# Attention's end, the pair products and the inverse root of a fused graph-attention kernel: another order of transfers and products, a shorter root

## The chip, the cores and the metric

One core of a Trainium2 chip. The metric is the device time of one execution, in microseconds (us): the median of 3 runs for the kernel before.

## The reference

With N = 4096 nodes and D = 512 features, `adj` a sparse 0/1 matrix [N, N], everything in fp32:

```python
q, k, v = x @ Wq.T + bq, key @ Wk.T + bk, value @ Wv.T + bv
s = (q @ k.T / N ** 0.5) * adj
s = where(abs(s) < 1e-5, -1e9, s)
x1 = layernorm(x + softmax(s) @ v @ Wm.T + bm)          # eps 1e-5
out = layernorm(x1 + relu((adj @ x1) @ W.T + b))        # eps 1e-5
```

`layernorm` subtracts the row's mean and divides by sqrt(variance + eps).

## The kernel before, in words

All products are made of 16-bit halves (a value is split in a high and a low part, three or two matmuls stand for one exact one). Node rows are worked in tiles of 128, n = 0 to 31. The program is written out by hand: every engine has its own instruction list, and semaphores tie them together. SP (`@block.sync`) and POOL (`@block.gpsimd`) issue the transfers, in the order in which they are written; a wait in such a list holds up all that stands behind it.

**Attention** takes 64 steps: 32 over the first half of the keys, then 32 over the second half (g = 32 + n). A step makes scores (L830), masks them and finds the row maximum (VectorE), takes exponentials and splits them in `Phl` (ScalarE, the high half, L1146; VectorE, the low half, L1529). SP turns both halves into `PT` by transposing transfers (`turn_prob`, L365 and L368) and TensorE weighs the values with them (`weigh`, L850). In the second half the two half results are merged, turned (`turn_merged`, L475 and L478) and projected (`project`, L871); the row is normalised to x1, split, turned (`turn_x1`, L462 and L465), stored (`store_x1`, L453), and multiplied with W1 (`rows_product`, L885), which gives the row Y[n]. `turn_x1(n)` waits until TensorE has used the turned row before it (semaphore `y_mm`). The adjacency is stored again in bf16 as it goes by (`store_adj`).

**Aggregation** makes adj @ Y for pairs of tiles (p, p + 16), p = 0 to 15. An adjacency tile (p, k) is 128 rows of 4096, turned from DRAM into SBUF in one transposing transfer (`adj_tile`, L483). Pairs 0 and 1 are made plainly (`aggregate`, L945, 64 matmuls a tile), pairs 2 to 15 with seven block products of 16 matmuls each instead of eight (`seven`, `product`, L976): VectorE makes four sums of adjacency blocks (`adj_sum`, L1892) and combines the products (`taken`, L1899, and `together`, L1904), and signed sums of Y rows (`Ta`, `Tb`) are made beforehand. `output` (L1847, L1851, L1854) and `result` (L1858 to L1863) then make the last layernorm of each tile.

**The order around the change.** POOL loads the rows of Y back in seven chunks of 4 tiles, 1 MB each (`load_y`), and the signed sums in three loads of 2, 2 and 1.5 MB (`load_sums`). Chunks 4, 5 and 6 wait for the last scores (`s_mm`), chunks 2 and 3 for the eleventh signed sums in DRAM; the first two sums loads for the last weighting (`o_mm`), the third for row 31's product (`y_mm`). In SP's last attention step (n = 31) tiles (0, 0) and (0, 1) stand ahead of `turn_prob`. After the loop come the last x row, row 29's turn, tile (1, 0), the last merged row, row 30's turn, the bias, tile (1, 1), row 31's turn.

TensorE's own list at attention's end is: `weigh(63)`, `rows_product(28)`, `project(62)`, the first parts of `aggregate(0, 0)` (32 matmuls), `rows_product(29)`, `project(63)`, 16 matmuls, `rows_product(30)`, 32 matmuls, `rows_product(31)`, then 176 matmuls for the rest of pairs 0 and 1, and `seven`. `seven` of the first pair waits until the fourth plain output has been read from PSUM (`f_out`). VectorE, after row 31's product, makes the last five signed sums (`joined`, `last_sums`, `signed_low`), three plain outputs with their results, four `adj_sum`, and the fourth output.

The inverse root is made on [128, 1] columns: three opening steps (add eps, a bit trick, scale) and three rounds of three instructions (L1608, L1610, L1611), 12 steps in all. In attention the steps are spread between VectorE's larger instructions (`score_chunks`); for the last rows and in `result` they run one behind the other.

In a pair, TensorE makes the products in the order 0, 1, 2, 3, 4, 5, 6. VectorE finishes the first tile's output after product 4 and the second tile's after product 6:

```python
dve.wait_ge(s_prod, 7 * q + 5)
taken(q, 5, csum[:, 1, :], u5[:, :], ps[:, 4, :], ALU.add)
output(u, 0, cs[:, 0, :], q + PLAIN)
result(u, 0)
dve.wait_ge(s_prod, 7 * q + 7)
taken(q, 7, csum[:, 0, :], u5[:, :], ps[:, 6, :], ALU.add)
taken(q, 9, u3[:, :], u2[:, :], ps[:, 6, :], ALU.add)
taken(q, 10, csum[:, 1, :], u3[:, :], ps[:, 5, :], ALU.subtract)
output(u + 1, 1, cs[:, 1, :], q + PLAIN)
```

## Time and profile before

| | |
|---|---|
| median of 3 runs | 2120.08 us (2117.37 to 2121.25) |
| the profiled execution | 2123.79 us |
| its span in the profile | 2122.1 us |
| TensorE busy | 2049.1 us, 97% |
| VectorE busy | 1487.2 us, 70% |
| ScalarE busy | 675.2 us, 32% |
| moved by the DMA engines | 359.57 MB, mean 169 GB/s |
| TensorE's slices below 9 tenths | 1st, 4th, 32nd and 40th (7 each), 34th (8) |

Times in the profile count from the start of the span. Matmuls are pipelined, so a busy TensorE need not be at its peak; a matmul's recorded duration is longer than the distance to the next one, and a group of matmuls is read by its length over its count. PEclk is the granted TensorE clock as a share of 2.4 GHz. In a timeline the bracket gives the idle time before an instruction and what ended it. [...]

### The profile page before, as it was taken

To read this page: it belongs to the slowest core of one execution; us is meant where nothing else is said; L and a number is where in the kernel's file an instruction comes from. 1 tells how busy PE (TensorE), PEld (TensorE's weight loads), DVE (VectorE), ACT (ScalarE), POOL (GpSimd) and SP (SyncE) were. 2 spreads that over 40 slices of the span, in tenths; PEclk is the share of its full clock that TensorE was granted. 3 is DMA by queue.
4 is the path that set the end of the run, shared out by engine and by line. 5 is a ranking of instruction groups with operands and counts; after the bars stand their busy time and mean duration, and the time that the engine had idled before them with its cause. 6 is when DMAs were issued, how large, how long until landed. Compare 5 with 4: busy or idle time off the path is not lost.

```text
span 2122.1 us, 30051 instructions
## 1 busy us (share of the span) xinstructions
PE 2049.1 (97%) x9471; PEld 981.9 (46%) x9471; DVE 1487.2 (70%) x3540; ACT 675.2 (32%) x884; POOL 81.1 (4%) x139
## 2 busy tenths in 40 slices
PE   7997999999999999999999999999999798999997
PEld 6773444444444444444444444444444333444443
DVE  3876656656565665687777777778888457888887
ACT  3443434344343434343333333343434110000000
POOL 1110000000000000000000000000000000000000
PEclk9998999999999999999999999999999899999999
DMA  7676777676667676887766666677777975555551
GB/s 243 230 267 150 189 176 155 168 168 162 162 161 182 148 173 155 224 168 163 164 163 160 163 165 165 162 176 184 187 185 208 256 174 119 134 124 119 133 138 56
DMA packets 586290, 359.57 MB, mean 169 GB/s; under 512 B 500992, under 2 KB 505088, under 8 KB 585856
## 3 DMA queue, kind: packets, MB, share of 16 engines
q1 hardware_dynamic: 564672, 275.07, 51.5%
q0 software_dynamic: 21568, 83.89, 16.3%
q8 instruction: 24, 0.39, 0.1%
q14 instruction: 26, 0.21, 0.0%
HBM read 181.15 MB, written 88.60 MB: 127 GB/s over the span
## 4 chain that ended last, share of the span: by engine, by line
PE 90%; DVE 5%; SPq 2%; DMA 2%; issue 1%; ACT 1%; DVEq 0%; ACTq 0%
PE ps L830 31%; PE ps L850 30%; PE ps L976 16%; PE ps L885 4%; PE ps L871 4%; PE ps L791 3%; SPq L483 1%; DMA wc<-in_L_gnn_Wv 1%; DMA x1T<-x1hl 1%; PE ps L775 1%; PE ps L945 0%; PE ps L738 0%; DMA stg<-in_L_gnn_value 0%; PE ps L804 0%; DVE mcol L1368 0%
## 5 line engine op out<-in xcount | busy, mean ns | idle before, releaser
L850 PE MATMUL ps<-V,PT 128*128 128x512 f16 x3072 | 676.3, 380 | 12.4 <-issue 12.4
L830 PE MATMUL ps<-KT,thl 128*128 128x512 f16 x3072 | 677.8, 381 | 9.6 <-DVE thl L1473 9.6
L850 PEld LDWEIGHTS ps<-V,PT 128*128 128x128 f16 x3072 | 301.1, 98 | 377.4 <-issue 17.2
L830 PEld LDWEIGHTS ps<-KT,thl 128*128 128x128 f16 x3072 | 301.5, 98 | 375.6 <-DVE thl L1473 10.7
L1500 DVE SCALAR_TENSOR_TENSOR prob<-ps,c_now,adjh 128x512 f32<-128x512 f32 x256 | 192.1, 751 | 289.1 <-PE ps L830 287.1
L1133 ACT ACTIVATE small<-prob 128x512 f32<-128x512 f32 x256 | 161.1, 630 | 631.4 <-DVE prob L1500 342.3
L1529 DVE SCALAR_TENSOR_TENSOR Phl<-prob,Phl 128x2048 f16<-128x2048 f32 x64 | 146.6, 2291 | 77.4 <-ACT Phl L1146 77.4
L1513 DVE CUSTOM_DVE_ANT_0 prob<-prob,small 128x512 f32<-128x512 f32 x256 | 174.5, 683 | 0.0
L1138 ACT ACTIVATE prob<-prob,nbias,inv 128x2048 f32<-128x2048 f32 x64 | 134.1, 2095 | 102.9 <-DVE nbias L1522 102.9
L1506 DVE TENSOR_SCALAR small<-small,eps_s,neg_s 128x512 f32<-128x512 f32 x256 | 139.0, 543 | 21.0 <-ACT small L1133 21.0
L1146 ACT ACTIVATE Phl<-prob 128x2048 f16<-128x2048 f32 x64 | 122.3, 1910 | 7.1
L1296 ACT ACTIVATE p<-ps 128x512 f32<-128x512 f32 x14 | 8.4, 597 | 335.5 <-DVE csum L1899 212.2
L976 PE MATMUL ps<-Y,AT 128*128 128x512 f16 x448 | 101.0, 384 | 6.4 <-DVE y L1847 6.4
L791 PE MATMUL ps<-xT,Aq 128*128 128x512 f32 x384 | 97.0, 403 | 1.8 <-DVE xT L1308 1.8
L885 PE MATMUL ps<-W1T,x1T 128*128 128x512 f16 x384 | 90.3, 386 | 6.6 <-DMA x1T<-x1hl 6.6
L871 PE MATMUL ps<-Wvm,UT 128*128 128x512 f16 x384 | 88.1, 379 | 1.1 <-issue 1.1
L672 POOL DMA_DIRECT2D adjh<-in_adj x64 | 36.1, 564 | 1388.5 <-DMA adj_bf<-adjh 826.6
L976 PE MATMUL ps<-Ta,S 128*128 128x512 f16 x336 | 79.4, 379 | 0.0
L976 PE MATMUL ps<-Tb,S 128*128 128x512 f16 x336 | 79.4, 379 | 0.0
L791 PEld LDWEIGHTS ps<-xT,Aq 128*128 128x128 f32 x384 | 71.1, 191 | 16.6 <-DVE xT L1308 2.5
L976 PEld LDWEIGHTS ps<-Y,AT 128*128 128x128 bf16 x448 | 44.2, 99 | 61.0 <-issue 9.5
L885 PEld LDWEIGHTS ps<-W1T,x1T 128*128 128x128 f16 x384 | 38.1, 99 | 53.7 <-DMA x1T<-x1hl 7.1
(179 smaller groups left out, 1765.1 us busy)
## 6 DMA issues: line engine op xcount, KB each, us to landing
adjh<-in_adj POOLq DMA_DIRECT2D x64, 512.0 KB, 5.3
adj_bf<-adjh SPq DMA_DIRECT2D x64, 512.0 KB, 4.4
t_in<-t_dram SPq DMA_DIRECT2D x64, 256.0 KB, 2.9
x_in<-in_x SPq DMA_DIRECT2D x64, 256.0 KB, 4.2
stg<-in_L_gnn_value POOLq DMA_DIRECT2D x12, 1024.0 KB, 7.3
rows<-in_x SPq DMA_DIRECT2D x32, 256.0 KB, 4.1
t_dram<-tq POOLq DMA_DIRECT2D x8, 1024.0 KB, 9.0
o_dram<-z_out SPq DMA_DIRECT2D x32, 256.0 KB, 2.8
```

Source lines behind the costliest of these rows:

```text
L791: last = nc.tensor.matmul(ps[:, BT + e, :], Aq[:, m, k, e * P:(e + 1) * P], xT[:, b, s, k, :], start=(n == 0), stop=(n == 3 * KD - 1))
L830: last = nc.tensor.matmul(ps[:, BS + c, :], thl[:, b, s, k * P:(k + 1) * P], KT[:, m, k, c * C:(c + 1) * C], start=(n == 0), stop=(n == 3 ...
L850: last = nc.tensor.matmul(ps[:, BU + b, :], PT[:, b, s, m, :], V[:, v, m, :], start=(m == 0 and q == 0), stop=(m == MT - 1 and q == 2))
L871: last = nc.tensor.matmul(ps[:, BZ, :], UT[:, b, s, k, :], Wvm[:, m, k, :], start=(n == 0), stop=(n == 3 * KD - 1))
L885: last = nc.tensor.matmul(ps[:, BY, :].rearrange("p (o n) -> p o n", n=P), x1T[:, s, k, :], W1T[:, m, :, k, :], start=(q == 0), stop=(q == ...
L976: last = nc.tensor.matmul(ps[:, bank, :].rearrange("p (s d) -> p s d", s=2), left(m), right(m), start=(m == 0), stop=(m == NP - 1))
L1133: nc.scalar.activation(small[:, c % 2, :], prob[:, b, c * C:(c + 1) * C], ACT.Abs).then_inc(s_abs, 1)
L1138: nc.scalar.activation(prob[:, b, :], prob[:, b, :], ACT.Exp, bias=nbias[:, b:b + 1], scale=inv[:, 0:1], accum_out=rsum[:, b:b + 1]).then_ ...
L1500: nc.vector.scalar_tensor_tensor(out=prob[:, b, c * C:(c + 1) * C], in0=ps[:, BS + c, :], scalar=c_now[:, b:b + 1], in1=adjh[:, b, c * C:( ...
L1506: nc.vector.tensor_scalar(small[:, c % 2, :], small[:, c % 2, :], eps_s[:, 0:1], neg_s[:, 0:1], ALU.is_lt, ALU.mult).then_inc(s_neg, 1)
L1513: nc.vector.tensor_tensor_reduce(out=prob[:, b, c * C:(c + 1) * C], in0=prob[:, b, c * C:(c + 1) * C], in1=small[:, c % 2, :], scale=1.0, ...
L1529: nc.vector.scalar_tensor_tensor(out=Phl[:, b, LO, :], in0=prob[:, b, :], scalar=P_SCALE, in1=Phl[:, b, HI, :], op0=ALU.mult, op1=ALU.subt ...
```

## The change

In SP's list, tile (0, 1) goes from before the last `turn_prob` to behind the last x row's load; tile (1, 0) from before the last merged row's turn to behind row 30's turn and store; row 31's turn and store go ahead of tile (1, 1). In POOL's list, chunks 4, 5 and 6 of Y wait for the last turned probabilities instead of the last scores, the first sums load for the last projection, the second for row 31's product. In a pair, products 4 and 6 change places, and with them the adjacency sums that they use and the two outputs: the second tile's output is now made after the sixth product, the first tile's after the seventh. The loads and stores of these tiles follow. The inverse root has three rounds of two instructions with other constants, 9 steps in all.

```diff
--- before.py
+++ after.py
@@ -24,9 +24,13 @@
 X_UP = 2.0 ** 9
 Y_DOWN = 2.0 ** -20
 
+
 ROOT_BITS = 0x7FFFFFFF
-ROOT_SCALE = 2.0 ** -65 / 1.4769
-ROOT_STEPS = 12
+ROOT_S2 = -0.5 ** (1 / 3)
+ROOT_S1 = (-ROOT_S2 / 2) ** (1 / 3)
+ROOT_S0 = -(ROOT_S1 / 2) ** (1 / 3)
+ROOT_SCALE = ROOT_S0 * 2.0 ** -65 / 1.4769
+ROOT_STEPS = 9
 
 
 def wait(eng, sem, value):
@@ -306,6 +310,10 @@
 
             return use % 2, 16 * (use // 2 + 1)
 
+        def place(p, k):
+
+            return 2 * p + (k if p < PLAIN else 1 - k)
+
         def before(b, j):
 
             return (0, j) if b == 1 else (1, j - 1)
@@ -515,9 +523,6 @@
                             sp.wait_ge(ab_st[k], 16 * (NT // 2 + NP // 2 + 1))
                         sp.wait_ge(p_lo, g)
                         adj_tile(0, 0)
-                        sp.wait_ge(ph_in[0], 16 * NT)
-                        sp.wait_ge(pl_in[0], 16 * NT)
-                        adj_tile(0, 1)
                     turn_prob(g, b)
                     if rows:
                         turn_x1(n - 3)
@@ -565,26 +570,30 @@
 
                 last = 2 * NT - 1
                 load_x_again(NT - 1, 1)
+
+                sp.wait_ge(ph_in[0], 16 * NT)
+                sp.wait_ge(pl_in[0], 16 * NT)
+                adj_tile(0, 1)
                 turn_x1(NT - 3)
                 store_x1(NT - 3, 1)
-                sp.wait_ge(p_lo, 2 * NT)
-                adj_tile(1, 0)
                 turn_merged(last, 1)
                 turn_x1(NT - 2)
                 store_x1(NT - 2, 0)
+                sp.wait_ge(p_lo, 2 * NT)
+                adj_tile(1, 0)
                 sp.wait_ge(y_st, 16 * (NT - TC))
                 sp.dma_start(b1_rep[:, :], b1.rearrange("(a n) -> a n", a=1).to_broadcast([P, D])).then_inc(s_bm, 16)
+                turn_x1(NT - 1)
+                store_x1(NT - 1, 1)
                 sp.wait_ge(ph_in[1], 16 * NT)
                 sp.wait_ge(pl_in[1], 16 * NT)
                 adj_tile(1, 1)
-                turn_x1(NT - 1)
-                store_x1(NT - 1, 1)
 
                 def load_row(p, k):
 
                     t = p + NP * k
                     if p > 0:
-                        sp.wait_ge(f_step, (ROOT_STEPS + 3) * (2 * (p - 1) + k) + 1)
+                        sp.wait_ge(f_step, (ROOT_STEPS + 3) * place(p - 1, k) + 1)
                     sp.dma_start(zf[:, k, :], x1_dram[t * P:(t + 1) * P, :]).then_inc(zf_in[k], 16)
 
                 for b in range(2):
@@ -607,9 +616,9 @@
                         for k in range(2):
                             load_row(p + 1, k)
 
-                for k in range(2):
+                for k in (1, 0):
                     t = NP - 1 + NP * k
-                    sp.wait_ge(f_res, NT - 1 + k)
+                    sp.wait_ge(f_res, place(NP - 1, k) + 1)
                     sp.dma_start(out[t * P:(t + 1) * P, :], y[:, k, :]).then_inc(last_st, 16)
                 sp.wait_ge(last_st, 32)
                 for k in range(2):
@@ -696,29 +705,30 @@
 
                 def store(p, k):
                     t = p + NP * k
-                    pool.wait_ge(f_res, 2 * p + k + 1)
+                    pool.wait_ge(f_res, place(p, k) + 1)
                     pool.dma_start(out[t * P:(t + 1) * P, :], y[:, k, :]).then_inc(out_st[k], 16)
 
 
                 pool.wait_ge(w_turned, 32)
                 for c in (0, 1):
                     load_y(c)
-                pool.wait_ge(s_mm, MC * 2 * NT)
+
+                pool.wait_ge(pl_in[1], 16 * NT)
                 for c in (4, 5, 6):
                     load_y(c)
                 pool.wait_ge(ts_st, 16 * EARLY)
                 for c in (2, 3):
                     load_y(c)
 
-                pool.wait_ge(o_mm, 2 * NT)
+                pool.wait_ge(z_mm, NT)
                 load_sums(0, Ta[:, 0:4, :, :, :])
+                pool.wait_ge(y_mm, NT)
                 load_sums(1, Ta[:, 4:8, :, :, :])
-                pool.wait_ge(y_mm, NT)
                 load_sums(2, Tb[:, 0:EARLY - 8, :, :, :])
                 for k in range(2):
                     store(0, k)
                 for p in range(1, NP - 1):
-                    for k in range(2):
+                    for k in range(2) if p < PLAIN else (1, 0):
                         store(p, k)
 
             @block.tensor
@@ -1017,14 +1027,14 @@
                     read(3)
                     product(3, adj_sum(1), signed(1))
                     pe.wait_ge(s_comb, 4 * q + 3)
-                    read(5)
-                    product(4, adj_sum(3), lower(1))
+                    read(7)
+                    product(6, adj_sum(2), signed(2))
                     pe.wait_ge(at_in[h][1], 16 * (turn + 1))
-                    read(10)
+                    read(8)
                     product(5, adj_block(h, 1, 1), signed(3))
                     pe.wait_ge(s_comb, 4 * q + 4)
-                    read(9)
-                    product(6, adj_sum(2), signed(2))
+                    read(10)
+                    product(4, adj_sum(3), lower(1))
 
                 for p in range(PLAIN, PLAIN + 2):
                     seven(p - PLAIN, p % 2, p // 2)
@@ -1604,11 +1614,10 @@
                                                        ALU.logical_shift_right, ALU.bitwise_xor)
                     if step == 2:
                         return nc.vector.tensor_scalar(r, r, ROOT_SCALE, None, ALU.mult)
-                    if step % 3 == 0:
+                    if step % 2 == 1:
                         return nc.vector.scalar_tensor_tensor(out=a, in0=r, scalar=v, in1=r, op0=ALU.mult, op1=ALU.mult)
-                    if step % 3 == 1:
-                        return nc.vector.tensor_scalar(a, a, -0.5, 1.5, ALU.mult, ALU.add)
-                    return nc.vector.tensor_tensor(r, r, a, ALU.mult)
+                    factor = -3.0 * (ROOT_S0, ROOT_S1, ROOT_S2)[step // 2 - 2] ** 2
+                    return nc.vector.scalar_tensor_tensor(out=r, in0=a, scalar=factor, in1=r, op0=ALU.add, op1=ALU.mult)
 
                 def inverse_deviation(n, b, step):
                     dve.wait_ge(r_step, (ROOT_STEPS + 2) * n + 2 + step)
@@ -1658,7 +1667,7 @@
                 def score_chunks(g, b, j, n=None):
 
                     def inverse(step):
-                        if n is not None:
+                        if n is not None and step < ROOT_STEPS - 1:
                             inverse_deviation(n, 1 - b, step)
 
                     masked(g, b, 0, j)
@@ -1881,7 +1890,7 @@
                                           for k in range(2) for half in range(2))
                     s1, s2, s3, s4 = S12[:, 0, :], S12[:, 1, :], S34[:, 0, :], S34[:, 1, :]
                     into, left, right, op, used, made = ((s1, a21, a22, ALU.add, 3, 0), (s2, s1, a11, ALU.subtract, 4, 1),
-                                                         (s3, a11, a21, ALU.subtract, 7, 0), (s4, a12, s2, ALU.subtract, 5, 2))[i]
+                                                         (s3, a11, a21, ALU.subtract, 5, 0), (s4, a12, s2, ALU.subtract, 7, 2))[i]
                     if i == 0:
                         for k in range(2):
                             dve.wait_ge(at_in[h][k], 16 * (turn + 1))
@@ -1891,7 +1900,7 @@
                         dve.wait_ge(s_comb, (4 * (q + 1) if q is not None else 0) + made)
                     nc.vector.tensor_tensor(into, left, right, op).then_inc(s_comb, 1)
 
-                for i in (0, 1, 3, 2):
+                for i in range(4):
                     adj_sum(i, None, PLAIN % 2, PLAIN // 2)
                 plain_output(1, 1)
 
@@ -1922,25 +1931,26 @@
                     taken(q, 4, u5[:, :], u2[:, :], ps[:, 2, :], ALU.add)
                     dve.wait_ge(s_prod, 7 * q + 5)
                     dve.wait_ge(c_step, 11 * q + 4)
-                    taken(q, 5, csum[:, 1, :], u5[:, :], ps[:, 4, :], ALU.add)
-                    together(q, 5, 1, 0, 1)
-                    dve.wait_ge(c_step, 11 * q + 6)
-                    output(u, 0, cs[:, 0, :], q + PLAIN)
+                    taken(q, 5, csum[:, 1, :], u5[:, :], ps[:, 6, :], ALU.add)
+                    together(q, 5, 1, 1, 1)
+                    taken(q, 7, u3[:, :], u2[:, :], ps[:, 6, :], ALU.add)
+                    dve.wait_ge(s_prod, 7 * q + 6)
+                    dve.wait_ge(c_step, 11 * q + 7)
+                    taken(q, 8, csum[:, 0, :], u3[:, :], ps[:, 5, :], ALU.subtract)
+                    together(q, 8, 0, 1, 0)
+                    dve.wait_ge(c_step, 11 * q + 9)
+                    output(u, 1, cs[:, 1, :], q + PLAIN)
+                    if nxt:
+                        adj_sum(2, q, *nxt)
+                    result(u, 1)
+                    dve.wait_ge(s_prod, 7 * q + 7)
+                    taken(q, 10, csum[:, 1, :], u5[:, :], ps[:, 4, :], ALU.add)
+                    together(q, 10, 1, 0, 1)
+                    dve.wait_ge(c_step, 11 * q + 11)
+                    output(u + 1, 0, cs[:, 0, :], q + PLAIN)
                     if nxt:
                         adj_sum(3, q, *nxt)
-                    result(u, 0)
-                    dve.wait_ge(s_prod, 7 * q + 7)
-                    taken(q, 7, csum[:, 0, :], u5[:, :], ps[:, 6, :], ALU.add)
-                    together(q, 7, 0, 1, 1)
-                    taken(q, 9, u3[:, :], u2[:, :], ps[:, 6, :], ALU.add)
-                    dve.wait_ge(c_step, 11 * q + 9)
-                    taken(q, 10, csum[:, 1, :], u3[:, :], ps[:, 5, :], ALU.subtract)
-                    together(q, 10, 1, 1, 0)
-                    dve.wait_ge(c_step, 11 * q + 11)
-                    output(u + 1, 1, cs[:, 1, :], q + PLAIN)
-                    if nxt:
-                        adj_sum(2, q, *nxt)
-                    result(u + 1, 1)
+                    result(u + 1, 0)
 
                 for p in range(PLAIN, PLAIN + 2):
                     pair(p - PLAIN, p % 2, p // 2, ((p + 1) % 2, (p + 1) // 2))
```

## Rows read from the trace of the kernel before

**Rows 1.** windows: us, busy us of each engine, PEclk (granted clock), DMA share, GB/s

```profile
1670.00:1676.00 6.00, 6.00 (x16) 2.08 (x15) 0.69 (x1) 0.63 (x1) 0.75 (x1) 0.53 0.70 165
1775.00:2100.00 325.00, 325.00 (x1508) 147.33 (x1506) 268.81 (x640) 8.36 (x14) 14.59 (x27) 1.00 0.52 123
```

**Rows 2.** TensorE's timeline: start, us, instructions [idle before, releaser]

```profile
1644.60 10.52 PE L850 MATMUL ps<-V,PT 128*128 128x512 f16 x48
...
1669.88 13.32 PE L850 MATMUL ps<-V,PT 128*128 128x512 f16 x48 [12.17 <-issue]
...
1701.90 4.92 PE L885 MATMUL ps<-W1T,x1T 128*128 128x512 f16 x12 [6.60 <-DMA x1T<-x1hl]
1707.88 2.75 PE L871 MATMUL ps<-Wvm,UT 128*128 128x512 f16 x12 [1.06 <-issue]
...
1723.42 2.75 PE L885 MATMUL ps<-W1T,x1T 128*128 128x512 f16 x12
1726.01 38.15 PE L945 MATMUL ps<-Y,AT 128*128 128x512 f16 x176
1770.53 9.05 PE L976 MATMUL ps<-Y,AT 128*128 128x512 f16 x32 [6.37 <-DVE y L1847]
```

**Rows 3.** timeline of SP's DMA queue: start, us to issue

```profile
1640.30 22.41 SPq L483 DMA_TRANSPOSE AT<-adj_bf  x2
1662.81 2.54 SPq L365 DMA_TRANSPOSE PT<-Phl  x1
...
1675.51 0.42 SPq L343 DMA_DIRECT2D x_in<-in_x  x1
...
1689.19 14.75 SPq L483 DMA_TRANSPOSE AT<-adj_bf  x1
...
1710.61 5.12 SPq L483 DMA_TRANSPOSE AT<-adj_bf  x1
```

**Rows 4.** timelines of ScalarE and VectorE: the last probabilities' two halves

```profile
1649.34 1.91 ACT L1146 ACTIVATE Phl<-prob 128x2048 f16<-128x2048 f32 x1
...
1651.28 2.29 DVE L1529 SCALAR_TENSOR_TENSOR Phl<-prob,Phl 128x2048 f16<-128x2048 f32 x1
```

**Rows 5.** DMA issues at 1640, 1710, 1686, 1665: last number, us to landing

```profile
AT<-adj_bf SPq DMA_TRANSPOSE x1, 19.1
...
AT<-adj_bf SPq DMA_TRANSPOSE x1, 8.6
...
x1T<-x1hl SPq DMA_TRANSPOSE x1, 15.6
...
PT<-Phl SPq DMA_TRANSPOSE x2, 4.5
```

**Rows 6.** windows of 2 us: DMA share and GB/s are the last two

```profile
1690.00:1692.00 2.00, 2.00 (x11) 0.93 (x10) 1.66 (x10) 0.00 (x0) 0.00 (x0) 1.00 1.01 422
1700.00:1702.00 2.00, 0.10 (x1) 0.11 (x2) 0.00 (x0) 0.07 (x1) 0.00 (x0) 0.50 1.14 234
```

**Rows 7.** VectorE's timeline: one inverse root of a plain output

```profile
1750.97 0.15 DVE L1601 TENSOR_SCALAR rv<-mv 128x1 f32<-128x1 f32 x1
...
1751.54 0.22 DVE L1608 SCALAR_TENSOR_TENSOR ra<-rstd,rv 128x1 f32<-128x1 f32 x1
1751.79 0.15 DVE L1610 TENSOR_SCALAR ra<-ra 128x1 f32<-128x1 f32 x1
...
1753.45 0.55 DVE L1863 TENSOR_SCALAR y<-y,mv,rstd 128x512 f32<-128x512 f32 x1
```

**Rows 8.** VectorE's timeline at the end of the run

```profile
2104.23 0.69 DVE L1899 TENSOR_TENSOR csum<-u,ps 128x512 f32<-128x512 f32 x1 [2.04 <-PE ps L976]
...
2110.43 0.55 DVE L1863 TENSOR_SCALAR y<-y,mv,rstd 128x512 f32<-128x512 f32 x1
2111.13 0.69 DVE L1899 TENSOR_TENSOR csum<-u,ps 128x512 f32<-128x512 f32 x1 [0.16 <-PE ps L976]
...
2119.10 0.55 DVE L1863 TENSOR_SCALAR y<-y,mv,rstd 128x512 f32<-128x512 f32 x1
```

## The prediction

> **What bounds the kernel now.** The page's busy shares come first: TensorE is busy for 97% of the span (the table above), so only its idle and slow stretches can be won. I looked for those. In the pair loop it is never idle: busy for 325.00 of 325 us at full granted clock, 1508 matmuls [rows 1]. A matmul costs 0.217 us at that clock (176 in 38.15 us, [rows 2]). VectorE is busy for 269 of those 325 us and has room. The long attention loops show no idle TensorE either, so fewer VectorE instructions there are worth nothing.
>
> The losses lie where attention ends. TensorE's timeline [rows 2] has four gaps: 12.17 us before the last weighting, 6.60 us before the product of row 29, 1.06 us before the last projection and 6.37 us before the seven products. After three of them it also runs slowly: the last weighting takes 13.32 us for 48 matmuls where the one before took 10.52 (+2.8), row 29's product 4.92 against 2.75 (+2.2), and 32 matmuls of the seven products 9.05 against 7.1 (32 x 0.217 and the last one's end; +2.0). The granted clock in 1670 to 1676 us was 0.53, the 1.2 GHz level, against 1.00 (2.4 GHz) in the loop [rows 1]; TensorE had been idle before it. The short gap of 1.06 us shows no slow stretch after it. Gaps and slow clock up to row 31's product come to 12.17 + 2.8 + 6.60 + 2.2 + 1.06 = 24.8 us.
>
> What causes them is in SP's queue [rows 3]. Two adjacency tiles hold it from 1640.30 to 1662.71 us, and the last probabilities are turned only behind them, at 1662.81. They were ready much earlier: ScalarE has the high half at 1651.25 and VectorE the low half at 1653.57 [rows 4]. The second gap ends with the turned row 29, issued at 1685.9 and landing 15.6 us later [rows 5]; POOL's bulk loads ran meanwhile, with 422 GB/s moved [rows 6]. The fourth gap is VectorE's: TensorE waits for the fourth plain output, whose first instruction ends at 1770.5.
>
> **Turns ahead of tiles.** Tile (0,0) stays in front of the last turn_prob, (0,1) goes behind it. A tile alone takes 5.12 us to issue [rows 3] and 8.6 us to land [rows 5]. Without the Y loads beside it, (0,0) is out of the queue by about 1646, before the probabilities. The low turn is issued at 1653.6 (some tenths earlier, since three small steps leave VectorE's path) and lands 4.5 us later [rows 5], at 1658.1. TensorE is free at 1657.71. The first gap shrinks from 12.17 to about 0.3 us, and I take its slow stretch as gone.
>
> The queue's work from there to row 31's x load took 13.1 us (1662.81 to 1675.93) [rows 3]; now it begins at 1651.3, waits for p_lo until 1653.6 and ends near 1663.2. Only then comes tile (0,1). POOL's loads of Y chunks 4 and 5 now wait for the turned probabilities (1658), chunk 6 for its rows, chunks 2 and 3 for the eleventh sums' store, near 1667. So tile (0,1) shares the DMA engines with about 3 MB of Y, 7.4 us at 422 GB/s, beside its own 5.1: the queue is free at 1675.7. The bound below is 5.12 (nothing shared), above 14.75 (the tile behind 6 MB, [rows 3]). Row 29's turns follow, 2.5 us of issue and about 2.4 us to land, at 1680 to 1682. TensorE needs them at 1657.7 + 0.3 + 104 matmuls x 0.217 = 1680.6 (weighting, row 28, projection, two parts of the first aggregate). I take 1.0 us of stall, ends 0 and 2.5. The last merged row follows in the queue; it needs the last x row, which is now loaded 12 us earlier, and is turned while TensorE works on row 29: no stall. The Y chunks needed at 1677 and 1686 are in by then: the queue of 5 MB that starts at 1658 is 12 us long at 422 GB/s; without that cover TensorE would wait for them us by us.
>
> **Tile (1,0) now stands between row 30 and row 31.** Row 30 is turned when row 29's product is done (1684), and lands ahead of TensorE's need at 1690. Then the tile is issued at about 1687.5, as the first sums load (2 MB, now behind the last projection) starts. Before, this tile's issue ended 3.6 us after the bulk had gone (1703.94, [rows 3], against about 1700.3, where the rate drops, [rows 6]). 2 MB at 422 GB/s are 5.0 us from 1688.6, so the tile is out at 1697.2; row 31's turns follow behind the bias load and land at 1702. TensorE needs them at 1699.4 (row 30's product, 8 and 24 matmuls of aggregates, with the 1.0 us above). Stall: 2.6 us, ends 0 (the tile takes 5.12) and 8 (it takes 14.75 less the overlap). Tile (1,1), now behind this row, has over 20 us until it is needed; so have the other sums loads, the first x1 rows and the tiles of the next pair.
>
> The Trainium skill (DMA: Bandwidth & Descriptors, Issuing engines are not separate DMA queues) speaks against the move: transfers of all issuing engines share the same 16 engines and interleave, so a later bulk load only meets other turns. The rows agree that turns and bulk disturb each other; the rule gives no price, and what it would make of the time is the third rival below.
>
> Sum to the end of row 31's product: -24.8 + 0.3 + 1.0 + 2.6 = -20.9 us.
>
> **Inverse root.** Now a root takes 2.48 us (1750.97 to 1753.45): three steps of 0.19 and three rounds of 0.25 + 0.19 + 0.19 [rows 7]. The new round has the same first instruction and one scalar_tensor_tensor with immediates. It is not shown: 0.19 like a small instruction with immediates, 0.25 like one with a per-partition scalar. I take 0.19, being the nearer kind, so a root saves 0.57 us (0.4 at the other end). VectorE's chain from row 31's product (end 1726.0) to the fourth output is 44.5 us long, TensorE's own work there 38.15 [rows 2]. Three roots lie in the chain: -1.7 us (-1.2 at the other end), leaving a gap of 4.7. The slow stretch behind it I leave at 2.0; none is the other end. The roots in attention and in the pair loop lie beside busy TensorE: 0. If TensorE ever waited for VectorE there, each would be worth 0.6.
>
> **Products in another order.** The number of matmuls and VectorE instructions is unchanged. By TensorE's needs product 6's adjacency sum is made 1 us into the next pair and needed at 13.9; product 4's by 9 us and needed at 20.9: no stall. SP's loads of x1 rows and POOL's stores follow the outputs' new order, with most of a pair's 24 us to spare. The tail changes. Now VectorE has finished the first output (2104.23 to 2110.98) just as TensorE ends, and then does csum, cs, u3 (1.79 us) and csum to result (to 2119.65) [rows 8]: 8.5 us. After, the three operations are one product earlier, but the first output starts with the last-but-one product, 3.5 us before TensorE's end, and takes 6.75 - 0.57 = 6.2 us: 2.7 us past the end. Then 6.73 - 0.57 = 6.2: together 8.9 us, +0.3. Ends -0.3 and +0.8.
>
> Sum: -20.9 - 1.7 + 0.3 = **-22.3 us**. The profiled execution took 2123.79 us, 3.7 over the median of 2120.08; I assume the stages' difference is the same and predict 2120.1 - 22.3 = 2097.8.
>
> **Rivals.** (1) All new stalls vanish: the tile shares little, and behind a gap of 4.7 us the clock comes back sooner. Then -20.9 - 3.9 - 1.7 + 0.3 - 2.0 = -28 at most, 2092; for it, a tile alone takes 5 us; against it, both tiles have bulk beside them. (2) One turn is still caught: row 31's low turn, issued at 1699.3, lands 14.6 us later as row 29's did, at 1714 instead of 1702. TensorE loses 12 us and 2.2 of slow clock: 2112. For it, the first sums load is near; against it, that load should be over by 1694. (3) **Slower:** bulk loads catch both turns. Row 29 lands 14.6 us after 1677, 11 us late, plus 2.2 slow; row 31 stands behind a tile of 14.75 us and lands 14.6 us later, 18.4 late, plus 2.2. Sum: -24.8 + 0.3 + 13.2 + 20.6 - 1.7 + 0.3 = +7.9, 2128. It decides from 26.2 us of new stalls and slow clock on (24.8 + 1.7 - 0.3). For it, the 15.6 us row; against it, only 3 and 2 MB stand where 6 did. (4) The probabilities stay late because tile (0,0) itself, landing after 19.1 us now [rows 5], holds them back: 1659.4 plus 4.5 leaves 6 us of the gap and a slow stretch of 2.5, 2106. Against it: two Y loads ran in those 19.1 us.
>
> **Numbers.** Forecast 0.57; all clear 0.19; one turn caught 0.12; probabilities late 0.07; slower 0.03; no difference 0.02. The range reaches from the best end of the first rival to the fourth, 2091.5 to 2107; the forecast's own is 2094 to 2102. About 0.2% (4.2 us) is what a measurement can tell from none: faster 0.95, same 0.02, slower 0.03.
>
> **What would show it.** The last weighting (L850) starts within 1 us of the projection before it, in full clock. Row 29's product has a gap under 2.5 us, row 31's is the one with the largest gap (0 to 5 us). The tile (1,0) takes about 10 us of SP's queue. The gap before the seven products is 4.5 to 5 us. A root takes 1.9 us. The tail from TensorE's last matmul to the last result is 8.9 us and TensorE stays unbroken in the pairs. A turned row that lands over 10 us after its issue, or any idle TensorE in the pair loop, would make the forecast wrong.

## The result, and the profile after

The changed kernel takes 2115.78 us, the kernel before 2120.69 (medians of 8 runs each): a ratio of 0.9969, interval 0.9955 to 0.9984 (the record's comparison of the runs, not the quotient of the two medians, which is 0.9977). That is 4.9 us less where 22.3 were forecast, outside the range. The two profiled executions are further apart than the medians: 2114.64 against 2123.79 us. The one of before lay 3.1 us over its median, the one of after 1.1 under. In the table further down one run of pool_only (2136.54 us) and one of y_early (2136.22) count as slow, so the ratios leave them out while the medians hold them.

Line numbers have moved by about 8 to 10: L850 is now L860, L885 L895, L871 L881, L945 L955, L976 L986, L483 L491, L365 L373, L462 and L465 are L470 and L473. The page's head:

```profile
span 2113.0 us, 29747 instructions
...
PE 2045.3 (97%) x9471; PEld 980.5 (46%) x9471; DVE 1464.9 (69%) x3348; ACT 675.2 (32%) x884; POOL 81.2 (4%) x139
```

TensorE's timeline of the changed kernel at attention's end, answering to [rows 2]:

```profile
1657.88 10.52 PE L860 MATMUL ps<-V,PT 128*128 128x512 f16 x48 [0.34 <-issue]
...
1671.45 2.75 PE L881 MATMUL ps<-Wvm,UT 128*128 128x512 f16 x12 [0.46 <-issue]
...
1692.09 5.30 PE L895 MATMUL ps<-W1T,x1T 128*128 128x512 f16 x12 [10.98 <-DMA x1T<-x1hl]
1697.18 2.88 PE L881 MATMUL ps<-Wvm,UT 128*128 128x512 f16 x12
...
1716.14 2.76 PE L895 MATMUL ps<-W1T,x1T 128*128 128x512 f16 x12 [3.13 <-DMA x1T<-x1hl]
1718.74 38.15 PE L955 MATMUL ps<-Y,AT 128*128 128x512 f16 x176
1761.40 8.75 PE L986 MATMUL ps<-Y,AT 128*128 128x512 f16 x32 [4.51 <-DVE y L1856]
```

The first gap is closed: 0.34 us instead of 12.17, and its slow stretch is gone. In its place row 29's product has a gap of 10.98 us instead of 6.60, and behind it 12 matmuls take 5.1 us where 2.6 is the full pace. Row 31's product has a new gap of 3.13 us. VectorE's gap before the seven products is 4.51 us instead of 6.37. They start at 1761.40 instead of 1770.53 us, and that is the whole difference of the spans (9.1 us).

SP's queue in the same stretch, answering to [rows 3]. An SPq line gives the start of an issue and how long the queue was held by it; tiles of one size hold it for 5.12 us [rows 3] and, here, 14.61, so this time includes waiting.

```profile
1639.89 6.17 SPq L491 DMA_TRANSPOSE AT<-adj_bf  x1
1650.89 1.32 SPq L373 DMA_TRANSPOSE PT<-Phl  x1
...
1665.63 14.61 SPq L491 DMA_TRANSPOSE AT<-adj_bf  x1
1680.37 7.09 SPq L470 DMA_TRANSPOSE x1T<-x1hl  x1
1687.56 2.46 SPq L473 DMA_TRANSPOSE x1T<-x1hl  x1
...
1700.65 10.74 SPq L491 DMA_TRANSPOSE AT<-adj_bf  x1
```

Tile (0,0) alone needs 6.17 us, and the last probabilities go out when they are made. Tile (0,1) now holds the queue for 14.61 us, and row 29's high turn behind it for another 7.09. The transfers' landing (last number, us from issue; tile (0,1), row 29's high turn, and the store of a Y row), answering to [rows 5]:

```profile
AT<-adj_bf SPq DMA_TRANSPOSE x1, 25.5
...
x1T<-x1hl SPq DMA_TRANSPOSE x1, 11.2
...
y_dram<-Yst SPq DMA_DIRECT2D x1, 256.0 KB, 9.2
```

Tile (0,1) is under way for 25.5 us. While it was, the DMA engines moved 248 GB/s on average at a busy share of 1.15. [rows 6] had shown both kinds of window: 422 GB/s at a share of 1.01 and 234 at 1.14. POOL's five Y chunks were issued at 1658.1, 1658.8, 1668.7, 1672.8 and 1673.6.

One inverse root of a plain output, answering to [rows 7]: 1743.69 to 1745.60, 1.91 us instead of 2.48. The new instruction with immediates takes 0.16 us:

```profile
1743.69 0.15 DVE L1611 TENSOR_SCALAR rv<-mv 128x1 f32<-128x1 f32 x1
...
1744.26 0.22 DVE L1618 SCALAR_TENSOR_TENSOR ra<-rstd,rv 128x1 f32<-128x1 f32 x1
1744.51 0.16 DVE L1620 SCALAR_TENSOR_TENSOR rstd<-ra,rstd 128x1 f32<-128x1 f32 x1
...
1745.60 0.55 DVE L1872 TENSOR_SCALAR y<-y,mv,rstd 128x512 f32<-128x512 f32 x1
```

The pair loop, in the window of 325 us, answering to the second row of [rows 1]: TensorE has no idle time, VectorE has 12 us less work:

```profile
1765.00:2090.00 325.00, 325.00 (x1505) 147.25 (x1504) 257.00 (x562) 8.36 (x14) 14.60 (x27) 1.00 0.51 124
```

The end of the run (TensorE's last product, then VectorE), answering to [rows 8]: TensorE ends at 2098.06 + 16 x 0.217 + 0.16 = 2101.7, the last result is made at 2110.51, 8.8 us later. Before, TensorE's last 8 matmuls started at 2109.21, so it ended at 2111.1 and the last result came 8.55 us later, at 2119.65.

```profile
2098.06 3.62 PE L986 MATMUL ps<-Y,S 128*128 128x512 f16 x16
...
2103.88 0.55 DVE L1872 TENSOR_SCALAR y<-y,mv,rstd 128x512 f32<-128x512 f32 x1
2104.34 0.68 DVE L1908 TENSOR_TENSOR csum<-u,ps 128x512 f32<-128x512 f32 x1
...
2109.96 0.55 DVE L1872 TENSOR_SCALAR y<-y,mv,rstd 128x512 f32<-128x512 f32 x1
```

### The profile page after: what moved, and what is told of

It is laid out like the page before. It is cut to its first block, busy times and chain, and to the rows that moved or that the text cites. A ratio compares the mean times of both kernels' runs of the same rounds, so it can differ in the third digit from the quotient of the medians.

```text
span 2113.0 us, 29747 instructions
## 1 busy us (share of the span) xinstructions
PE 2045.3 (97%) x9471; PEld 980.5 (46%) x9471; DVE 1464.9 (69%) x3348; ACT 675.2 (32%) x884; POOL 81.2 (4%) x139
## 4 chain that ended last, share of the span: by engine, by line
PE 88%; DVE 5%; SPq 3%; DMA 3%; ACT 1%; issue 1%; DVEq 0%; ACTq 0%
PE ps L840 31%; PE ps L860 29%; PE ps L986 16%; PE ps L895 4%; PE ps L881 4%; PE ps L801 2%; SPq L491 1%; DMA stg<-in_L_gnn_value 1%; DMA wc<-in_L_gnn_Wv 1%; PE ps L785 1%; SPq L470 1%; PE ps L748 0%; DVE mcol L1378 0%; DMA x1T<-x1hl 0%; SPq L373 0%
## 5 line engine op out<-in xcount | busy, mean ns | idle before, releaser
L860 PE MATMUL ps<-V,PT 128*128 128x512 f16 x3072 | 673.5, 379 | 0.6 <-issue 0.6
L860 PEld LDWEIGHTS ps<-V,PT 128*128 128x128 f16 x3072 | 300.4, 98 | 363.5 <-issue 1.9
L1516 DVE TENSOR_SCALAR small<-small,eps_s,neg_s 128x512 f32<-128x512 f32 x256 | 138.9, 543 | 20.9 <-ACT small L1143 20.9
L986 PE MATMUL ps<-Y,AT 128*128 128x512 f16 x448 | 100.7, 384 | 4.5 <-DVE y L1856 4.5
L895 PE MATMUL ps<-W1T,x1T 128*128 128x512 f16 x384 | 90.7, 387 | 14.1 <-DMA x1T<-x1hl 14.1
L881 PE MATMUL ps<-Wvm,UT 128*128 128x512 f16 x384 | 88.2, 379 | 0.5 <-issue 0.5
L986 PE MATMUL ps<-Ta,S 128*128 128x512 f16 x336 | 79.4, 379 | 0.0
L986 PE MATMUL ps<-Tb,S 128*128 128x512 f16 x336 | 79.4, 379 | 0.0
L986 PEld LDWEIGHTS ps<-Y,AT 128*128 128x128 bf16 x448 | 44.2, 99 | 58.9 <-issue 7.2
L895 PEld LDWEIGHTS ps<-W1T,x1T 128*128 128x128 f16 x384 | 38.0, 99 | 61.5 <-DMA x1T<-x1hl 15.1
```

Source lines behind the costliest of these rows:

```text
L860: last = nc.tensor.matmul(ps[:, BU + b, :], PT[:, b, s, m, :], V[:, v, m, :], start=(m == 0 and q == 0), stop=(m == MT - 1 and q == 2))
L881: last = nc.tensor.matmul(ps[:, BZ, :], UT[:, b, s, k, :], Wvm[:, m, k, :], start=(n == 0), stop=(n == 3 * KD - 1))
L895: last = nc.tensor.matmul(ps[:, BY, :].rearrange("p (o n) -> p o n", n=P), x1T[:, s, k, :], W1T[:, m, :, k, :], start=(q == 0), stop=(q == ...
L986: last = nc.tensor.matmul(ps[:, bank, :].rearrange("p (s d) -> p s d", s=2), left(m), right(m), start=(m == 0), stop=(m == NP - 1))
L1516: nc.vector.tensor_scalar(small[:, c % 2, :], small[:, c % 2, :], eps_s[:, 0:1], neg_s[:, 0:1], ALU.is_lt, ALU.mult).then_inc(s_neg, 1)
```

## Experiments

"Changed" and "before" are the two kernels of this document. Where a time is called less or more it is against the kernel before in the same group of runs (2122 to 2124 us). Gaps are those of one profiled execution each. In the profiles TensorE begins the projection of row 62, before the first gap, anywhere from 1653.3 to 1655.4 us, so a start of the seven products that differs by 2 us says nothing by itself.

| kernel | median us (runs) | ratio, interval | first gap | row 29 | projection 63 | row 30 | row 31 | seven products at |
|---|---|---|---|---|---|---|---|---|
| before (profile above) | 2120.69 (8) | 1 | 12.17 | 6.60 | 1.06 | 0 | 0 | 1770.5 |
| changed | 2115.78 (8) | 0.9969, 0.9955 to 0.9984 | 0.34 | 10.98 | 0 | 0 | 3.13 | 1761.4 |
| after_again | 2118.20 (10) | 0.9989, 0.9978 to 0.9999 | 0.31 | 10.48 | 0 | 0 | 3.91 | 1760.6 |
| tile01_later | 2106.81 (4) | 0.9915, 0.9889 to 0.9941 | 0.30 | 5.62 | 1.39 | 3.75 | 0 | 1759.4 |
| tiles_later | 2104.38 (4) | 0.9904, 0.9878 to 0.9930 | 0.31 | 0 | 3.54 | 3.60 | 0 | 1752.0 |
| y_late | 2107.93 (4) | 0.9921, 0.9895 to 0.9947 | 0.33 | 0 | 0 (then 4.20) | 1.52 | 2.28 | 1754.1 |
| y_early | 2124.48 (10) | 0.9989, 0.9964 to 1.0013 | 0.82 | 14.45 | 0 | 0 | 4.03 | 1766.9 |
| tile01_back | 2109.04 (6) | 0.9939, 0.9917 to 0.9961 | 1.14 | 0 | 0.27 | 0 | 3.07 | 1749.1 |
| pool_only | 2105.54 (4) | 0.9918, 0.9889 to 0.9948 | 0.78 | 0 | 4.68 | 0 | 0.44 | 1752.2 |
| root_only | 2112.83 (8) | 0.9956, 0.9941 to 0.9970 | 6.38 | 5.98 | 0.90 | 0 | 0 | 1760.4 |
| pair_only | 2125.41 (12) | 1.0012, 0.9998 to 1.0026 | 15.47 | 6.85 | 1.39 | 0 | 0 | 1773.5 |
| order_root12 | 2121.11 (10) | 0.9999, 0.9982 to 1.0016 | 0.58 | 10.09 | 0 | 0 | 3.71 | 1764.2 |
| y_shift | 2120.39 (10) | 0.9996, 0.9983 to 1.0009 | 6.62 | 9.32 | 0.91 | 0 | 0 | 1765.6 |
| best | 2098.44 (4) | 0.9887, 0.9870 to 0.9904 | 0.92 | 0 | 0.70 | 0 | 0 | 1745.8 |

**What delays row 29's turn.** The first group takes the tile away from in front of it, or the bulk loads away from beside the tile.

tile01_later:

```diff
                 load_x_again(NT - 1, 1)
-                sp.wait_ge(ph_in[0], 16 * NT)
-                sp.wait_ge(pl_in[0], 16 * NT)
-                adj_tile(0, 1)
                 turn_x1(NT - 3)
                 store_x1(NT - 3, 1)
                 turn_merged(last, 1)
+                sp.wait_ge(ph_in[0], 16 * NT)
+                sp.wait_ge(pl_in[0], 16 * NT)
+                adj_tile(0, 1)
                 turn_x1(NT - 2)
```

> The changed kernel with tile (0,1) behind the last merged row's turn; nothing else. Theory A (row 29's turn is late because it stands in SP's queue behind a tile that bulk loads slow down): row 29's gap on TensorE falls from 10.98 us to under 1 and its slow stretch of 2.5 goes; the seven products start 11 to 13 us earlier; time about 2104. Rival B (chunks of Y hold up any turn, whatever stands ahead of it): row 29's turns are issued near 1672 but land 8 us or more later, the gap stays over 3 us. Rival C (the tile only moves on): row 30's turn, now behind the tile, gets a gap of 5 us or more.

Measured: 2106.81 us. The profiled execution was the slowest of its four (2113.92; the others 2105.64 to 2107.78), and it shows what is left:

```profile
1685.62 5.06 PE L895 MATMUL ps<-W1T,x1T 128*128 128x512 f16 x12 [5.62 <-DMA x1T<-x1hl]
1692.06 2.75 PE L881 MATMUL ps<-Wvm,UT 128*128 128x512 f16 x12 [1.39 <-DMA UT<-Uhl]
...
1702.01 5.30 PE L895 MATMUL ps<-W1T,x1T 128*128 128x512 f16 x12 [3.75 <-DMA x1T<-x1hl]
```

Row 29's turns were issued at 1670.6 and 1671.9, free of the tile, and still landed 10.3 and 13.7 us later, beside the Y chunks of 1668.6 and 1672.4. Row 29's gap fell from 10.98 to 5.62 us, by half, not under 1 us as theory A expected, and the seven products start only 2.0 us earlier; B's sign (a landing 8 us or more later, a gap over 3) came true: the chunks alone can cost a turn 8 to 11 us. The other three runs are 6 to 8 us faster than the profiled one and may hold a smaller gap; they have no profile. Row 30 has a gap of 3.75 us, below C's 5. The tile held its turns back, and the low one, issued at 1694.8 with the first sums load at 1695.1, also landed late.

tiles_later is tile01_later with `adj_tile(1, 0)` and its wait moved down as well:

```diff
-                sp.wait_ge(p_lo, 2 * NT)
-                adj_tile(1, 0)
                 sp.wait_ge(y_st, 16 * (NT - TC))
...
                 turn_x1(NT - 1)
                 store_x1(NT - 1, 1)
+                sp.wait_ge(p_lo, 2 * NT)
+                adj_tile(1, 0)
                 sp.wait_ge(ph_in[1], 16 * NT)
```

> The changed kernel with all turned rows ahead of tiles: (0,1) behind the last merged row, (1,0) behind row 31's turn. Theory A: no gap over 1 us before rows 29, 30 or 31, the seven products start 15 to 17 us earlier than in the changed kernel, time about 2100. Rival C (transfers only change places): the tiles (1,0) and (1,1) land late, and the plain aggregate of pair 1 waits 3 us or more, time no less than with tile (0,1) moved alone.

Measured: 2104.38 us. Rows 29 and 31 have no gap; the merged row and row 30 have:

```profile
1685.96 2.75 PE L881 MATMUL ps<-Wvm,UT 128*128 128x512 f16 x12 [3.54 <-DMA UT<-Uhl]
...
1695.76 2.76 PE L895 MATMUL ps<-W1T,x1T 128*128 128x512 f16 x12 [3.60 <-DMA x1T<-x1hl]
```

Row 29's turns stand in the same place as in tile01_later and landed after 6.5 and 7.9 us instead of 10.3 and 13.7: two profiles of the same meeting. The merged row's turns, issued at 1676.1 and 1677.5 beside chunks 2 and 3, took 9.3 and 8.4 us to land. Row 30's low turn, issued at 1688.7 as the first sums load started (1689.0), took 7.0. The expectation of no gap over 1 us was wrong at row 30, the seven products start 9.4 us earlier and not 15 to 17, and the time is 4 us above the 2100 expected. Rival C's gap in the plain aggregates does not appear, but something of it does: the gap before the seven products is 6.00 us instead of 4.51, since VectorE waited 1.40 us for the store of an earlier result, issued while SP's next two tiles took 20.32 us of queue.

y_late keeps all of SP's order and takes the chunks away from the tile:

```diff
-                for c in (4, 5, 6):
+                for c in (4, 5):
                     load_y(c)
                 pool.wait_ge(ts_st, 16 * EARLY)
-                for c in (2, 3):
+                pool.wait_ge(y_mm, NT - 2)
+                for c in (2, 3, 6):
                     load_y(c)
```

> The changed kernel with chunks 2, 3 and 6 of Y behind row 29's product, so that only chunks 4 and 5 can be beside tile (0,1). Theory A: the tile's issue falls from 14.6 us to 5 to 8, row 29's turns land by 1680, the gap of 11 us falls under 1; TensorE then waits 3 to 8 us for chunks 2 and 3; time 3 to 8 us less. Rival E (the tile is slow by itself, or by chunks 4 and 5): its issue stays over 11 us and row 29's gap over 7.

Measured: 2107.93 us, 10 us under the changed kernel run later on the same chip (2118.20). SP's queue, then TensorE:

```profile
1665.17 8.99 SPq L491 DMA_TRANSPOSE AT<-adj_bf  x1
1674.29 1.19 SPq L470 DMA_TRANSPOSE x1T<-x1hl  x1
```

```profile
1689.91 5.43 PE L956 MATMUL ps<-Y,AT 128*128 128x512 f16 x16 [4.20 <-DMA Y<-y_dram]
```

The tile needs 8.99 us instead of 14.61 and row 29's high turn 1.19 instead of 7.09; row 29's gap is gone. TensorE then waits 4.20 us for the chunks. Theory A holds, rival E falls. The tile's issue came out above the 5 to 8 expected; chunk 5, the second of the two issued from 1657.4 on, landed after 11.0 us, some 4 us into the tile.

y_early undoes one of POOL's waits in the changed kernel:

```diff
-                pool.wait_ge(pl_in[1], 16 * NT)
+                pool.wait_ge(s_mm, MC * 2 * NT)
```

> The changed kernel with POOL's wait for chunks 4, 5 and 6 as before (last scores made). Theory A (the volume of bulk beside tile (0,1) decides): only chunks 6, 2 and 3 are left beside the tile and come earlier, its issue falls from 14.6 us to 8 to 11, row 29's gap from 11 to 3 to 6, time 5 to 8 us less. Rival D (the new wait is what closes the first gap): chunks 4 and 5 slow down tile (0,0) to 12 us or more, the last probabilities land late, the last weighting gets a gap of 3 us or more again, and the time is the same or longer.

Measured: 2124.48 us, and scattered from 2104.63 to 2136.22. Neither expectation held. The first gap stayed closed, so D falls: with one tile ahead, which took 6.04 us of queue, the probabilities are in time even with two chunks beside it. But the tile (0,1) was slower, not faster:

```profile
1664.36 18.42 SPq L491 DMA_TRANSPOSE AT<-adj_bf  x1
1682.89 7.75 SPq L470 DMA_TRANSPOSE x1T<-x1hl  x1
```

```profile
1658.46 10.52 PE L860 MATMUL ps<-V,PT 128*128 128x512 f16 x48 [0.82 <-issue]
...
1695.52 4.88 PE L895 MATMUL ps<-W1T,x1T 128*128 128x512 f16 x12 [14.45 <-DMA x1T<-x1hl]
```

Chunk 6 was issued at 1663.65 here and chunks 2 and 3 at 1667.6, so all 3 MB were issued between 0.7 us before and 4 us after the tile (in the changed kernel 3 to 8 us after it). In this execution the same volume cost the tile 4 us more by coming earlier, and the tile landed only after 30.1 us. The whole change without this one wait of POOL's is worth nothing measurable.

**What made the first gap.** The second group asks whether the place of tile (0,1) or the chunks beside it closed the first gap.

pool_only, made from the kernel before:

```diff
-                pool.wait_ge(s_mm, MC * 2 * NT)
+                pool.wait_ge(pl_in[1], 16 * NT)
...
-                pool.wait_ge(o_mm, 2 * NT)
+                pool.wait_ge(z_mm, NT)
                 load_sums(0, Ta[:, 0:4, :, :, :])
-                load_sums(1, Ta[:, 4:8, :, :, :])
                 pool.wait_ge(y_mm, NT)
+                load_sums(1, Ta[:, 4:8, :, :, :])
```

> The kernel before with POOL's new waits alone (chunks 4, 5 and 6 after the last turned probabilities, the sums loads later); both tiles stay ahead of the last probabilities. Theory F (the first gap came from the Y chunks beside the two tiles, not from the tiles' place): without them the two tiles take about 10 us of SP's queue instead of 22.4 and are out by 1651, the gap of 12.17 us falls under 2, and since row 29's turn has no tile before it, its gap is under 4; time 12 to 18 us less than before, and less than the changed kernel's. Rival G (a tile's place decides): the first gap stays over 6 us.

Measured: 2105.54 us, 18 us less than before, with 12 root steps and the old order of tiles. SP's queue, then TensorE:

```profile
1639.24 11.06 SPq L483 DMA_TRANSPOSE AT<-adj_bf  x2
```

```profile
1657.34 10.52 PE L850 MATMUL ps<-V,PT 128*128 128x512 f16 x48 [0.78 <-issue]
...
1687.21 4.44 PE L871 MATMUL ps<-Wvm,UT 128*128 128x512 f16 x12 [4.68 <-issue]
```

Both tiles together take 11.06 us instead of 22.41 [rows 3] and are out of the queue at 1650.30, before the probabilities are made. Theory F holds: without the two Y chunks beside them both tiles can stay in their place. Together with y_early, which closed the same gap by moving one tile with the chunks left where they were, this says that the gap needed both, two tiles in front and two chunks beside them; removing either is enough. POOL's part of the change alone gives over three times what the whole change gives. It holds two things, the chunks' wait and the sums loads' waits. The first gap lies before the sums loads, so the chunks closed it; what of row 29's gap (6.60 us, now 0) is due to which was not taken apart.

tile01_back is the changed kernel with the first three lines of tile01_later's diff put back ahead of the last `turn_prob`, as before.

> The changed kernel with tile (0,1) back ahead of the last probabilities. Theory F: first gap under 2 us, row 29's gap under 3 instead of 10.98; the seven products start 9 to 13 us earlier than in the changed kernel. Rival G: the last weighting gets a gap of 6 us or more and nothing is won over the changed kernel.

Measured: 2109.04 us (2101.74 to 2115.68). In the profiled execution, one of the two fastest, the first gap is 1.14 us, row 29 has none, and the seven products start 12.3 us earlier than in the changed kernel. Theory F again, with both its signs; what the scatter of the others holds was not profiled.

**The other parts.** root_only is the kernel before with the diff's root (constants, steps and the guard in `score_chunks`) and nothing else.

> The kernel before with the inverse root in 9 steps alone. Expected by the prediction's term: a root takes 1.91 us instead of 2.48, the chain from row 31's product to the seven products is 1.7 us shorter, the tail 0.6 us shorter, all else equal: 2 us less, which the time may not tell. Rival: in attention the missing steps move VectorE's other work and the turned rows fall otherwise beside the bulk loads, so that the gaps change by more than the root.

Measured: 2112.83 us, 10.7 less, where 2 were expected: the rival holds. A root takes the expected 1.9 us and VectorE's gap falls to 4.65 us, but the larger part is in the transfers. SP's queue, then TensorE:

```profile
1638.36 15.84 SPq L486 DMA_TRANSPOSE AT<-adj_bf  x2
```

```profile
1662.38 13.01 PE L853 MATMUL ps<-V,PT 128*128 128x512 f16 x48 [6.38 <-issue]
...
1693.47 5.08 PE L888 MATMUL ps<-W1T,x1T 128*128 128x512 f16 x12 [5.98 <-DMA x1T<-x1hl]
```

The same two tiles take 15.84 us of the queue instead of 22.41, so the first gap is 6.38 instead of 12.17 us. The seven products start 10.2 us earlier: 5.8 from this gap, 1.7 from VectorE's, 0.6 from row 29's, 0.3 from slow clock and a projection, and 1.7 because the projection of row 62 came earlier, which is not the root's doing, since y_shift has it as well without the root. SP had started them 2.4 us ahead of the Y chunks instead of 2.2.

y_shift tests this on the kernel before, with no arithmetic changed:

```diff
-                pool.wait_ge(s_mm, MC * 2 * NT)
+                pool.wait_ge(s_adj, MC * 2 * NT)
```

> The kernel before with chunks 4, 5 and 6 of Y waiting for the last masked scores instead of the last scores, 0.7 us later; nothing else. Rival I (how the chunks meet the two tiles decides, and root_only won 10.7 us by starting the tile 0.2 us earlier against them): the two tiles' issue falls from 22.4 us to 15 to 18, the first gap from 12 to 6 to 9, the time by 5 us or more. Theory H: nothing changes within 2 us.

Measured: 2120.39 us. The chunks start 3.0 us behind the tiles:

```profile
1638.77 16.67 SPq L483 DMA_TRANSPOSE AT<-adj_bf  x2
```

```profile
1662.81 12.83 PE L850 MATMUL ps<-V,PT 128*128 128x512 f16 x48 [6.62 <-issue]
...
1697.05 5.02 PE L885 MATMUL ps<-W1T,x1T 128*128 128x512 f16 x12 [9.32 <-DMA x1T<-x1hl]
```

The tiles take 16.67 us and the first gap is 6.62 us, as rival I expected; 2.7 us of that was lost again at row 29, whose gap grew to 9.32 us, and the time moved by 1.8 us, less than the 5 us expected and not clear of noise. So where two tiles and two chunks meet, a shift of 0.2 to 0.9 us went with 6 us of the tiles' issue, in one profile of each kernel. That this is also the whole of root_only's 10.7 us is argued, not shown: its gap at row 29 was not longer, and why stays open.

pair_only is the kernel before with the diff's changes to `seven`, `adj_sum`, `pair`, and the loads and stores that go by `place`; the root has 12 steps.

> The kernel before with the other order of a pair's products alone (root in 12 steps). By the prediction's working the tail from TensorE's last matmul to the last result is csum to y of the first output, 3.25 us of it past TensorE's end, then 6.73: 9.9 to 10.1 us against 8.6 before, so 1.3 us longer, and TensorE unbroken in the pairs. Rival: a result that is made one product earlier shortens the tail by the three operations, 1.8 us.

Measured: 2125.41 us, no difference that the runs can tell. Its first gap is 15.47 us, again by the two tiles (25.58 us of queue, started 2.1 us ahead of the chunks), which this part does not touch. TensorE is unbroken in the pairs. VectorE's end:

```profile
2116.62 0.55 DVE L1869 TENSOR_SCALAR y<-y,mv,rstd 128x512 f32<-128x512 f32 x1
2117.08 0.68 DVE L1905 TENSOR_TENSOR csum<-u,ps 128x512 f32<-128x512 f32 x1
...
2123.26 0.55 DVE L1869 TENSOR_SCALAR y<-y,mv,rstd 128x512 f32<-128x512 f32 x1
```

TensorE ends at 2113.85, the last result at 2123.81: 9.96 us against 8.55 before, within the 9.9 to 10.1 expected. The three operations are one product earlier, but the second tile's result, until 2117.17, now lies past TensorE's end. The rival falls.

order_root12 is the changed kernel with the root of before.

> The changed kernel with the inverse root in 12 steps again. Theory H (the root is worth its VectorE time): 1.7 us longer chain before the seven products and about 0.6 us of tail, so 2.3 us more than the changed kernel, gaps at rows 29 and 31 the same within 1 us. Rival I (the root shifts when transfers meet, as with root_only): the gaps at rows 29 to 31 differ by 4 us or more in sum, either way.

after_again is the changed kernel itself, in the same group.

> The changed kernel once more, beside the others of this group. If its traces repeat, row 29's gap is again 9 to 13 us, the tile (0,1) takes 13 to 16 us of SP's queue, and the time is 5 to 8 us under the kernel before. If it lies at 2104 or under, the comparison of the first runs was of one chip only.

Measured: 2121.11 and 2118.20 us, 2.9 apart, with gaps at rows 29 and 31 within 0.4 us of each other and VectorE's gap 6.25 against 4.53. With the transfers' meetings the same, VectorE's gap shows the root's 1.7 us; the times fit the 2.3 us of theory H, though their ranges overlap (2117.88 to 2128.65, 2113.92 to 2122.98). The changed kernel repeated its gaps; its time was 4.0 us under the kernel before here and 4.9 in the first runs, less than the 5 to 8 expected.

**A kernel that beats both.** best is tile01_back with tiles_later's second edit: both tiles of pair 0 ahead of the last probabilities, POOL's new waits, both tiles of pair 1 behind row 31's turn.

> The changed kernel with tile (0,1) in its old place ahead of the last probabilities and tile (1,0) behind row 31's turn. By theories A and F together: first gap about 1 us, no gap over 1 us at row 29, under 3 at row 31, seven products near 1746; about 2099 to 2103, the fastest so far. If bulk loads beside turns decide whatever the tiles do, rows 30 or 31 get a gap of 3 us or more and it is no faster than tiles_later.

Measured: 2098.44 us (2096.43 to 2100.02), ratio 0.9887, with the gaps as expected. Its TensorE timeline:

```profile
1659.03 10.52 PE L860 MATMUL ps<-V,PT 128*128 128x512 f16 x48 [0.92 <-issue]
...
1684.97 2.75 PE L881 MATMUL ps<-Wvm,UT 128*128 128x512 f16 x12 [0.70 <-DMA UT<-Uhl]
...
1703.10 38.15 PE L955 MATMUL ps<-Y,AT 128*128 128x512 f16 x176
1745.78 9.75 PE L986 MATMUL ps<-Y,AT 128*128 128x512 f16 x32 [4.53 <-DVE y L1856]
```

Between the last weighting and the seven products the gaps are 0.92 and 0.70 us. What is left is VectorE's chain (4.53 us and a slow stretch behind it).

## Why the prediction was wrong

**Right, first gap.** 0.3 us forecast, 0.34 measured, slow stretch gone. But only half of the cause was read: I saw two tiles in front of the probabilities and took their place for the cause. The Y loads came in only as what would no longer run beside tile (0,0); I did not ask what holding them back was worth by itself. pool_only closes the gap with both tiles in place, y_early with both chunks in place. The row to read was their 22.41 us against 5.12 for a tile alone [rows 3]: 12 us of the 22 came from what ran beside them.

**The step that failed: "I take 1.0 us of stall, ends 0 and 2.5" for row 29.** It failed because the turns behind tile (0,1) were priced as if they ran alone. It measured 10.98 us and a slow stretch of 2.5. The sum to the end of row 31's product was forecast at -20.9 us and came out at -7.3; of the 13.6 us between them 12.6 are this term, 0.5 row 31's, 0.5 a short gap at a projection. The term was wrong in three places, each seen in rows of the changed kernel. The tile was issued at 1665.63 instead of 1663.2, since the turns and stores before it met chunks 4 and 5 (the two turns of the merged row took 1.70 and 2.32 us of queue, 1.23 and 1.50 before). It took 14.61 us instead of 12.5; the upper bound of 14.75 was right, but it led to a stall of 2.5 us only because I let the turns behind the tile go at 1.25 us each and land after 2.4. They took 7.09 and 2.46 us of queue, and the high one 11.2 us to land, at 1691.6, half a microsecond after the tile, which was under way for 25.5 us. A queue that is free to issue is not a queue that is empty. y_late shows that the bulk loads were behind it: with chunks 2, 3 and 6 held back and SP's order unchanged, the tile took 8.99 us, the high turn 1.19 and the gap was gone. And the way the price was worked out, volume over 422 GB/s plus the tile's own time, has no term for this: while the tile was under way the trace has 248 GB/s, and y_early, with the same 3 MB, had 169 and took 18.42 us. [rows 6] held the warning, a window with full engines and 234 GB/s, which was read as the bulk being gone. One of the prediction's own signs of being wrong, a turned row that lands over 10 us after its issue, came true here.

The second rival (one turn caught, 0.12) and the third had the mechanism; the second had it for row 31 and put the time at 2112. The third priced row 29 at 11 us and 2.2 of slow clock (10.98 and 2.5 measured), and row 31 at 18.4 (3.13 measured). I took the two as one case and gave it 0.03, while each tile meets its own loads: one caught and one not was the result.

**Right, row 31.** 2.6 us forecast, 3.13 measured; the tile (1,0) took 10.74 us of the queue, about 10 expected. (By the prediction's own counts TensorE would need the row at 1699.8 and not 1699.4, 84 matmuls after 1681.6, which makes 2.2 us.) Its gap has no slow stretch behind it, and there is some luck in that: after_again and order_root12 had 3.91 and 3.71 us with 1.7 us of slow clock behind them.

**Right, root and VectorE's chain.** 1.91 us a root, the immediate form at the cheaper end. The chain from row 31's product to the seven products is 42.66 us instead of 44.52: -1.86 for -1.7. The slow stretch behind it shortened by 0.3. That nothing would be won elsewhere held for the changed kernel (order_root12), not for the kernel before, where the root moved the meeting of transfers (root_only).

**Right, the pairs.** TensorE unbroken; the tail 0.3 us longer (8.83 against 8.55), 0.3 forecast; pair_only shows 1.4 us with the longer root, where its working gives 1.3.

**Interleaving.** The Trainium skill (DMA: Bandwidth & Descriptors, Issuing engines are not separate DMA queues) says that transfers of all issuers interleave on the same engines. The runs agree: with three more Y chunks issued by POOL beside it, SP's tile took 14.61 us instead of 8.99 (changed kernel, y_late). For the tile I had it as a term, too small; for the turns behind the tile only as a rival.

**From the profile to the median.** The spans differ by 9.1 us, the medians by 4.9. The working used one execution of before that was 3.1 us over its median. Of the 17.4 us by which the forecast missed, 13.2 (22.3 less 9.1) lie between the two profiles, and 4.2 in how far these two executions lie from their medians. The runs of after_again reach from 2113.9 to 2123.0, with gaps made by meetings that vary. One profile of such a stretch is a sample.

## What to carry to other kernels

Before moving a transfer that stands in front of a late one, compare its issue time with the same transfer's where nothing runs beside it: if it is several times longer, try holding back the neighbour as well as moving the transfer. When a large tile is put ahead of a small turned one, cost the small one by the tile's landing and not by its issue, and ask what the bulk queue will be doing then. A change that wins by closing one gap should be tried in parts: here one part alone (pool_only, 18 us) gave more than the whole (4.9 us), and putting tile (0,1) back (tile01_back) won 7 to 9 us over the changed kernel, so two of the parts worked against each other.
